# Dividing the attention sums in the transposed layout on VectorE, and taking half of the exponents head by head from PSUM, in a fused tokenizer, attention and expert kernel

## The reference, cut to what matters

```
b, t, dim = x.shape                      # 64, 82, 256
H, hd = 16, 16
qkv = (xn @ w_qkv + b_qkv)
scores = jnp.einsum('bhqd,bhkd->bhqk', q, k) * scale
attn = jax.nn.softmax(scores + bias, axis=-1)
out = jnp.einsum('bhqk,bhkd->bhqd', attn, v)
out = jnp.transpose(out, (0, 2, 1, 3)).reshape(b, t, dim)
return out @ w_out + b_out
```

## Time and profile before

| | us |
|---|---|
| median of 3 runs | 630.31 (628.71 to 632.13) |
| the profiled execution | 628.26 |
| its span, first to last instruction | 626.1 |
| PE busy / PEld busy / DVE busy / ACT busy | 584.7 / 496.4 / 491.0 / 386.4 |
| the batch loop, from the score matmuls of b = 2 (start 133.89) to those of b = 63 (end about 492.4) | 358.5 |

### The profile page before, as it was taken

How to read it: one execution, slowest core, us unless ns; L and a number is a source line. 1 busy time by engine, 2 the same in 40 slices (tenths; PEclk the granted TensorE clock), 3 DMA queues, 4 the chain that set the end, 5 groups by cost and what they waited for, 6 DMA issues and landing times.

```text
span 626.1 us, 21143 instructions
## 1 busy us (share of the span) xinstructions
PE 584.7 (93%) x8306; PEld 496.4 (79%) x8306; DVE 491.0 (78%) x1021; ACT 386.4 (62%) x867; POOL 311.6 (50%) x401
## 2 busy tenths in 40 slices
PE   9999989799999999999999999999999889999940
PEld 8788868568888878888888888888888778889830
DVE  2666868789989899899989898988887666666516
ACT  1222134157677667777776677677767767887724
POOL 1587772428757678688884324433111214344430
PEclk9999999899999999999999999999999999999985
DMA  8999004110111116314434331111151225554439
GB/s 305 382 346 329 6 9 126 48 51 20 36 44 54 61 51 181 113 54 135 128 113 135 95 89 43 44 53 49 39 80 52 61 52 120 119 103 112 86 120 324
DMA packets 59212, 68.42 MB, mean 109 GB/s; under 512 B 27020, under 2 KB 45708, under 8 KB 58604
## 3 DMA queue, kind: packets, MB, share of 16 engines
q1 hardware_dynamic: 54652, 57.73, 31.4%
q0 software_dynamic: 4464, 9.35, 5.0%
HBM read 31.06 MB, written 25.21 MB: 90 GB/s over the span
## 4 chain that ended last, share of the span: by engine, by line
PE 67%; DVE 7%; issue 4%; ACT 1%; DMA 1%; POOL 1%; SPq 0%; POOLq 0%; DVEq 0%
PE psQ L1351 11%; PE psQ L1319 10%; PE psS L1342 7%; PE psO L1361 7%; PE psS L1471 6%; PE psQ L1329 5%; PE psO L1486 5%; PE psQ L1385 5%; PE psO L1369 4%; DVE mx L1769 2%; PE psQ L1456 2%; PE psO L1376 1%; PE psQ L1499 1%; PE psQ L1310 1%; DVE qk_space L1757 1%
## 5 line engine op out<-in xcount | busy, mean ns | idle before, releaser
L1611 ACT ACTIVATE probT<-psQ 82x328 f32<-82x328 f32 x256 | 110.2, 438 | 21.3 <-PE psQ L1351 19.6
L1769 DVE TENSOR_REDUCE mx<-psS 82x8 f32<-82x656 f32 x128 | 106.0, 828 | 11.5 <-PE psS L1342 11.1
L1351 PE MATMUL psQ<-ident_all,prob 82*82 82x82 f32 x1024 | 113.4, 236 | 1.0 <-DVE qk_space L1757 0.6
L1351 PEld LDWEIGHTS psQ<-ident_all,prob 82*82 82x82 f32 x1024 | 89.6, 120 | 28.7 <-issue 7.1
L1771 DVE TENSOR_TENSOR prob<-psS,mx 82x656 f32<-82x656 f32 x128 | 107.1, 836 | 4.4
L1603 ACT ACTIVATE prob<-prob 82x656 f32<-82x656 f32 x128 | 94.9, 742 | 4.3 <-DVE prob L1771 3.4
L1203 POOL TENSOR_TENSOR big<-big,po 128x256 f32<-128x256 f32 x41 | 30.0, 732 | 129.5 <-ACT po L1598 129.2
L1319 PE MATMUL psQ<-hT,wqkv 128*128 128x328 f32 (+10 forms) x320 | 81.4, 388 | 0.0
L1264 POOL DMA_INDIRECT entry_rows<-yv,slot_entry x39 | 39.7, 1018 | 54.0 <-ACT yv L1656 48.2
L1581 ACT ACTIVATE oT<-psO 128x328 f32<-128x328 f32 x64 | 28.4, 444 | 54.1 <-PE psO L1361 54.1
L1807 DVE COPY qk_space<-ex_weights 64x640 f32 x78 | 39.6, 508 | 26.2 <-PE psQ L1499 24.5
(11 more groups left out here) (278 smaller groups left out, 1149.3 us busy)
## 6 DMA issues: line engine op xcount, KB each, us to landing
slot_rows<-xh SPq DMA_DIRECT2D x1, 4992.0 KB, 32.5
fused_rows<-in_txt SPq DMA_DIRECT2D x1, 4928.0 KB, 19.8
vv<-vs SPq DMA_DIRECT2D x24, 164.0 KB
big<-in_patches SPq DMA_DIRECT2D x2, 1600.0 KB, 11.6
out<-big SPq DMA_DIRECT2D x25, 128.0 KB, 3.1
big<-entry_rows SPq DMA_DIRECT2D x6, 512.0 KB, 7.2
ex_weights<-in_wa SPq DMA_DIRECT2D x8, 320.0 KB
ex_weights<-in_wb SPq DMA_DIRECT2D x8, 320.0 KB
```

Of the source, the lines that this page charges most:

```text
L1351: mm = te.transpose(bank(("turn", 4 * b + g))[0:T, s * T:s * T + T], prob[:, b % 2, g, s, :], ident_all[0:T, 0:T])
L1611: act.activation(probT[:, b % 2, g, :, :].rearrange("p s t -> p (s t)"), bank(("turn", 4 * b + g))[0:T, 0:4 * T], ACT.Copy).then_inc(S["pr ...
L1769: v.tensor_reduce(mx[:, half, :, :], s4, X, ALU.max).then_inc(S["max_ready"], 1)
```

## The change

On the way of the sums: `turn_back`, `turn_att`, `copy_oT`, `copy_attT` and `normalise` go. `weigh` now writes the 16 heads into one bank as two halves, a = 0 in columns 0 to 163 and a = 1 in columns 192 to 355, with the head pairs of 32 rows laid so that the values of one and the ones of the other take the upper and the lower 16 rows. VectorE turns the bank in blocks of 32x32 (`turn_sums`), takes the reciprocal of 12 columns, turns these, spread over 16 rows each, back into the layout of the sums (`divide`), lays the second half over the first half's copy where a mask says so, and multiplies. ScalarE copies the first half (`copy_sums`). psO is released by the masked copy (`sums_read`).

On the way of the exponents: for the first eight heads of each batch VectorE only takes the (negated) maxima, and ScalarE computes exp(score + (-maximum)) straight from psS, one instruction for each head, with the maximum as bias: two times four instructions (`exponent_heads(b, 0)` and `(b, 1)`), placed before the second and after the second copy probT. The other eight heads stay as they were.

```diff
             def turn(b, g):
-                te.wait_ge(S["prob_ready"], 2 * b + g // 2 + 1)
+                if g < 2:
+                    te.wait_ge(S["heads_ready"], 2 * b + g + 1)
+                else:
+                    te.wait_ge(S["prob_ready"], b + 1)
...
             def weigh(b):
                 te.wait_ge(S["probT_ready"], 4 * b + 4)
                 te.wait_ge(S["v_in%d" % (b % 4)], 16 * v_pieces[b])
-                te.wait_ge(S["attT_ready"], b)
...
+                te.wait_ge(S["sums_read"], b + 1)
+                for t in range(2):
+                    for a in range(2):
+                        for g in range(HG):
+                            mm = te.matmul(psO[32 * g:32 * g + 32, SW * a + T * t:SW * a + T * t + T], vv[:, b % 4, 8 * t + 2 * g + a, :],
+                                           probT[:, b % 2, g, 2 * t + a, :], start=True, stop=True, tile_position=(0, 32 * g))
                 mm.then_inc(S["weigh_done"], 1)
-            def turn_back(b):
-                te.wait_ge(S["oT_ready"], b + 1)
-                for s in range(4):
-                    mm = te.transpose(psO[0:T, s * 128:s * 128 + 128], oT[:, s, :], ident_all[:])
-                mm.then_inc(S["back_done"], 1)
-            def turn_att(b):
-                te.wait_ge(S["att_ready"], b + 1)
-                for c in range(2):
-                    mm = te.transpose(psO[:, c * T:c * T + T], att[:, 8 * c:8 * c + 8, :].rearrange("p h d -> p (h d)"), ident_all[0:T, 0:T])
-                mm.then_inc(S["attT_ps"], 1)
...
+            def copy_sums(b):
+                act.wait_ge(S["den_turned"], b + 1)
+                if b >= 2:
+                    act.wait_ge(S["attT_ready"], b - 1)
+                act.activation(sums[:, b % 2, :], psO[:, 0:2 * T], ACT.Copy).then_inc(S["sums_copied"], 1)
...
+            def exponent_heads(b, g):
+                act.wait_ge(S["max_ready"], 2 * b + 1)
+                if b >= 2:
+                    act.wait_ge(S["turn_done"], 4 * (b - 2) + g + 1)
+                for s in range(4):
+                    ins = act.activation(prob[:, b % 2, g, s, :], psS[0:T, g, s * T:s * T + T], ACT.Exp, bias=mx[:, 0, g, s:s + 1])
+                ins.then_inc(S["heads_ready"], 1)
...
+            def turn_sums(b):
+                v.wait_ge(S["weigh_done"], b + 1)
+                v.transpose(den_turned[:], psO[:, 0:2 * SW]).then_inc(S["den_turned"], 1)
+            def divide(b):
+                v.wait_ge(S["den_turned"], b + 1)
+                dens = den_turned[:, HD:HD + 2 * (SW - HD)].rearrange("p (a n) -> p a n", a=2)[:, :, 0:SW - HD:32]
+                v.reciprocal(rden[:], dens).then_inc(S["rden_ready"], 1)
+                v.wait_ge(S["rden_ready"], b + 1)
+                v.transpose(share[:].rearrange("p (j a d) -> p j a d", a=2, d=HD),
+                            rden[:].rearrange("p a j -> p j a").unsqueeze(3).to_broadcast([128, SW // 32, 2, HD])).then_inc(S["share_ready"], 1)
+                v.wait_ge(S["sums_copied"], b + 1)
+                v.copy_predicated(sums[:, b % 2, :], odd_rows[:].bitcast(I32), psO[:, SW:SW + 2 * T]).then_inc(S["sums_read"], 1)
...
+                    ins = v.tensor_tensor(attT[:, :, a:a + size], sums[:, b % 2, :].rearrange("p (c t) -> p c t", c=2)[:, :, lo:lo + size],
+                                          share[:, 0:2 * T].rearrange("p (c t) -> p c t", c=2)[:, :, lo:lo + size], ALU.mult)
+                ins.then_inc(S["attT_ready"], 1)
```

More of the change, by code:

```diff
@@ L1010, in attention_and_experts @@
         prob = prob_all[0:T, :].rearrange("p (r g s t) -> p r g s t", r=2, g=HG, s=4); probT = sb("probT", [T, 2, HG, 4, T])
-        oT = sb("oT", [128, 4, T]); att = sb("att", [T, NH, HD])
-        attT = sb("attT", [128, 2, RA]); rden = sb("rden", [T, NH, 1])
+        attT = sb("attT", [128, 2, RA])
+        SW = 192
+        sums = sb("sums", [128, 2, 2 * T]); odd_rows = sb("odd_rows", [128, 2 * T])
+        den_turned = sb("den_turned", [128, 2 * SW]); rden = sb("rden", [128, 2, SW // 32]); share = sb("share", [128, SW])
         po = sb("po", [128, 2, C])
@@ L1543, in _ @@
             low(1)
-            turn_back(NB - 1)
             project(NTL - 2)
-            turn_att(NB - 1)
             project(NTL - 1)
@@ L1574, in copy_val @@
                         act.wait_ge(S["v_in%d" % (k % 4)], 16 * v_pieces[k])
-                act.activation(vs[:, n % RV, :, 0:HD], bank(("val", n))[:, 0:C].rearrange("p (h d) -> p h d", h=NH),
+                own_half = vs[:, n % RV, :, :].rearrange("p (m a) (k d) -> p m (a k) d", a=2, k=2)[:, :, 0:4:3, :]
+                act.activation(own_half, bank(("val", n))[:, 0:C].rearrange("p (m a d) -> p m a d", a=2, d=HD),
                                ACT.Copy).then_inc(S["psQ_act"], 1)
[L1578 to L1591, removed]
+            def copy_sums(b):
[3 more added lines that the diff above has]
+                act.activation(sums[:, b % 2, :], psO[:, 0:2 * T], ACT.Copy).then_inc(S["sums_copied"], 1)
             def copy_project(n):
@@ L1690, in _ @@
                     copy_val(n)
+                exponent_heads(b, 0)
                 if b >= 1:
                     copy_probT(b - 1, 1)
-                exponent(b, 0)
+                if b >= 2:
+                    copy_sums(b - 2)
+                exponent_heads(b, 1)
                 for n in projected(b):
@@ L1877, in _ @@
                 normal_stats(n)
+            v.wait_ge(S["proj_read"], 22)
+            v.memset(psO[:, 0:2 * SW], 1.0).then_inc(S["sums_read"], 1)
+            v.tensor_copy(odd_rows[:], own[:, 1:2].to_broadcast([128, 2 * T]))
             owners = {}
@@ L1883, in _ @@
                 shift(b, 0)
+                if b >= 2:
+                    turn_sums(b - 2)
                 shift(b, 1)
                 if b >= 2:
-                    normalise(b - 2)
+                    divide(b - 2)
                 for n in turned(b + 2):
@@ L1901, in _ @@
             owners[1] = experts(1)
-            normalise(NB - 2)
+            turn_sums(NB - 2)
+            divide(NB - 2)
             own_wb(0, owners[0])
             own_wa(1, owners[1])
-            normalise(NB - 1)
+            turn_sums(NB - 1)
+            divide(NB - 1)
             for p in range(NPAIR):
```

46 lines of the change are left out of this document (19 added, 27 removed).

## The result

The changed kernel takes 653.88 us (median of 4 runs, 650.39 to 654.75) against 629.51 for the kernel before (median of 4 runs): a ratio of 1.039 with a 95% interval of 1.0342 to 1.0437, 24.4 us more. The forecast was slower, 652 us, 21 more than before. The profiled execution takes 654.75, its span 652.6 (before 626.1).

What follows compares the result with a forecast made beforehand. TensorE bounded the kernel before; the ring would bound the changed one: 5.40 us plus 0.82 of tile work is 6.22 against 5.88, 0.34 x 62 = +21 us, so 630.3 becomes 652. Range 617 to 672, the forecast's own 641 to 662.

Steps and rivals of the forecast that it cites:

- The ring: Loop over TensorE and ScalarE: fourth probT, weigh, turn, first probT, ScalarE's round; 6.22 us on average against 5.88 before.
- The handoff: Part of the loop iteration from fourth probT through weigh and turn to the next first probT; 1.70 us.
- Four heads: Four of the eight small exponents on ScalarE, between first and fourth probT; 0.92 us, at 0.23 each.
- A round with project alone: Loop iteration whose only tile work is project: 5.40 us without tile work, 0.29 more for po; 5.69 forecast.
- the mean of 6.22: Average loop iteration: 5.40 us without tile work plus 0.82 on average for tile work, over 62 iterations.
- The price of a small exponent: Start to start on ScalarE, 0.23 us for one 82-column exponent with operand, 1.84 for eight; lower bound 1.04, upper 2.0.
- 1.67 us were forecast: VectorE's five new instructions in a loop iteration, against 1.38 removed; its work would be 5.55 us an iteration.
- the rival with the double price: VectorE becomes the bound, turns or masked copy taking two passes; 6.7 us an iteration at most, 680 us; chance 0.08.
- TensorE is off the bound: In the loop TensorE is spared 0.68 us an iteration, needs 5.20, and idles about 1 us, mostly before weigh.
- The 588 of this rival: TensorE, by occupancy, stays the measure and all 42 us come back: 588 us; strongest form of the faster rival, chance 0.20.
- The waits added for psS and psO: In the loop, new waits for these banks cost nothing as long as VectorE's work stays under the 6.22 us iteration.
- The tail: After the loop, two rounds of turns go (1.4 us) while VectorE's last chain grows by as much; taken as nothing.

Runs made afterwards that it cites:

- copy_in_gap: The changed kernel with one more ScalarE copy of 128x512 in each iteration, placed behind the fourth probT; ratio to the kernel before 1.032.
- copy_in_ring: The changed kernel with one added ScalarE copy of 128x512 per iteration, behind the eighth head, between first and fourth probT; ratio to the kernel before 1.092.
- heads_only: The kernel before with only the exponents of eight heads moved to ScalarE, head by head, and its old division kept; 655.69 us, ratio 1.043.
- one_exponent: The changed kernel with one exponent of 82x656 from psS, no maximum subtracted, in place of the eight small ones; 615.93 us, ratio 0.981.
- division_only: The changed kernel with the new division on VectorE, but the eight heads given back their subtraction and single exponent; 665.65 us, ratio 1.058.
- shared_shift: The changed kernel with one maximum per row over the eight heads and one exponent with that bias; 612.67 us, ratio 0.972.
- weigh_later: The changed kernel with TensorE's weigh(b-2) put behind turn(b-1, 0) instead of ahead of it; 643.88 us, ratio 1.023.
- changed_again: The changed kernel unaltered, measured once more for the spread; 654.56 us, ratio to the kernel before 1.041.
- shared_shift_all: The changed kernel with one maximum per row for each group of eight heads, no VectorE subtraction, second exponent before the third probT; 616.84 us, ratio 0.979.

## Why the prediction was right, point by point

**The ring became the bound: right.** The wait moved to the first probT; copy_in_gap and copy_in_ring show that work between the first and the fourth probT counts and work in the gap doesn't; heads_only shows that moving the exponents is enough for the loss, and one_exponent that one cheap exponent in place of the eight turns it into a gain.

**Its terms.** The handoff was taken as 1.70 and is 1.79 (343.74 to 345.53). Four heads were taken as 0.92 and take 0.84 and 0.85, 0.21 each instead of 0.23. A round with project alone: 5.69 forecast, 5.54 measured; with xT and val 6.43 and 6.31; with all three 6.72 and 6.58 (338.95 to 345.53). So each was 0.12 to 0.15 too large, mostly the heads. From b = 18 to 59 the iterations average 6.10 where the terms give 6.24; the mean of 6.22 was met because the first 16, b = 2 to 18, take 6.58 (6.30 before), with work in them that is in no term. These first 16 lengthen by 0.28 each, the later 41 by 0.34. That the average agrees to 0.01 is partly luck.

**The price of a small exponent.** The groups of after give 340 ns with the bias, and the starts lie 0.21 us apart. The Trainium skill's rule of the section on the TRN2 errata, on the page "VectorE: DVE Perf Modes", weighed in the prediction, gave 0.21 us for one and, less the overlap, 0.11 from start to start, about half of it; it has no term for the operand. The Trainium skill's page "ScalarE: Activation LUTs" (section "What ACT_TABLE_LOAD costs") says that each per-partition operand adds about 93 ns. The trace roughly agrees: 226 ns for a copy of 72 columns without one, 340 for an exponent of 82 with one, 114 more, of which some belongs to the ten further columns.

**VectorE: right.** 1.67 us were forecast and 1.64 measured, the two turns with 0.51 and 0.30 against 0.50 and 0.30, so the rival with the double price is out. VectorE lies under the ring in after, and is the bound when it has more to do (division_only). With a shorter ring (shared_shift) it is near the bound; whether it is the bound isn't shown.

**TensorE is off the bound: right; how far, was not.** Its busy time should have fallen by some 40 us and fell by 12.4 over the 59 iterations, while that of its weight loads fell by 33.8; the pauses shown come to 0.59 us an iteration (367 less 332.3, over 59), not about 1. Nor is the one before `weigh` the largest, as forecast: in the loop's 367 us the scores wait 12.4 us for the exponents, and `weigh` 8.7 for probT, though by the order of events above it is the latter that ends last. Busy is the time in which a matmul is under way. Where matmuls stand less close, each shows with its full length instead of the part before the next: from `qk` to the turn behind it are 1.32 us in the round with project alone (347.31 to 348.63), 1.14 in before (343.75 to 344.89). That this is all of the difference is argued, not shown, and so is TensorE's 5.20 itself: the shortest loop of all runs has 5.62. By the Trainium skill's page "Perfetto Trace Analysis" (section "Identifying the Most-Contended Engine") the engine with the highest occupancy comes first, with TensorE judged by its weight loads. The prediction read this as speaking for TensorE. In the loop it doesn't: the weight loads are busy 300.7 of 358.5 us (84%) and VectorE 320.3 (89%), so VectorE would come first. The 588 of this rival is the prediction's own sum of 630 less 42, not the page's. TensorE was relieved, and the kernel got 4% slower; heads_only relieved VectorE, and was as slow. Occupancy doesn't show the ring.

**The waits added for psS and psO cost nothing: right for after, at the edge.** Scores wait 0.6 for the eighth head, and this is hidden, since the fourth probT comes 0.38 later still. VectorE waits more for ScalarE's copy of the sums (14.3 us from 135 to 480) than for the scores (5.2), which the prediction named. weigh_later shows that the edge is near.

**The tail was taken as nothing: this term was wrong,** 7.4 us. It had turns and VectorE's last chain in it, and nothing for the clock, which was 0.81, 0.51, 0.66 and 0.83 in the four stretches of 10 us from 500 on. So the profiled execution is 5 us above the forecast for it (649.7 against 654.75); the medians are nearer (652 and 653.88), since this execution lies 0.9 above its median and that of before 2.05 below. changed_again (0.83, 0.66, 0.77 and 0.88 in the four stretches) and weigh_later (0.50 for 20 us) show the same fall. Against before's, the end is 6.0 us longer in changed_again, 2.6 in heads_only (0.83 and 0.85 at the lowest) and 2.0 in shared_shift (0.83 over 20 us), but only 0.4 in shared_shift_all, although its clock falls too (0.91, 0.84 and 0.74 in the stretches from 470 to 500). So the fall of the clock alone doesn't set it. Which part of the 7.4 is the clock and which the waits, and the val that came late at b = 61, no run takes apart.

## What to carry to other kernels

When two engines hand work to each other in program order, add up one round along the handoffs before you add up any engine's work: here the busiest engine had two steps, 0.68 us together, taken off every iteration, and the kernel got slower, since other work was put inside a ring that had only a few tenths of a microsecond of slack. Work in the gap of the handoff was nearly free (a copy of 0.5 us left the ratio at 1.03), and the same work inside the round cost its full price (1.09). Three new orders opened the ring, and each only ran into the next wait; a cheaper operation inside the ring was worth more here. Eight small exponents with an operand each took 1.69 us, where one of 656 columns took 0.59 without an operand and 0.69 with one.

## What the runs showed of the hardware that was not expected

The granted clock fell from 1.00 to 0.50 at the loop's end, came back twice for a few microseconds, and stayed at 1.00 only from 534 on. The eight other kernels whose windows were read there show a fall too, from 0.91 over 20 us (one_exponent) to 0.50 over 20 us (weigh_later), and before shows none. The same instruction doesn't always take the same time: probT takes 0.44 us at the start of a round in after and 0.49 on both sides of the last exponent, and this exponent of 656 columns takes 0.80, where before has 0.43 to 0.44 and 0.74. VectorE's product of 128x164 takes 0.33 us in the rounds shown, while one in shared_shift at 348.96 takes 0.78 and one in reordered at 354.86 takes 1.07. No run explains these.
